# A graph layer, a mixture of experts and a second graph layer on one core: neighbouring tokens put side by side in a partition

## What is computed

```
x = x + (A @ (LN(x) @ W0 + b0)) / deg[:, None]          # A = adj != 0, deg = column sums
x = x + MoE(LN(x))        # 8 experts 256 -> 1024 -> 256, gelu, top 2 of a softmax gate
x = x + relu(D^-1/2 (A + I) D^-1/2 @ LN(x) @ WL.T + bL)
x = x + nibble_shift(LN(x))   # reads columns 0, 39, 40, 64..111, adds to columns 128..159
```

## Time and profile before

| | us |
|---|---|
| median of 3 runs | 1022.38 |
| the profiled execution, its own time | 1022.8 |
| its span, first to last instruction | 1021.0 |
| TensorE busy in the span | 929.0 |

### The profile page before, as it was taken

How to read it: one execution, slowest core, us unless ns; L and a number is a source line. 1 busy time by engine, 2 the same in 40 slices (tenths; PEclk the granted TensorE clock), 3 DMA queues, 4 the chain that set the end, 5 groups by cost and what they waited for, 6 DMA issues and landing times. The chain is left out here.

```text
span 1021.0 us, 21671 instructions
## 1 busy us (share of the span) xinstructions
PE 929.0 (91%) x6625; PEld 608.5 (60%) x6626; DVE 590.0 (58%) x1878; ACT 400.7 (39%) x837; POOL 429.6 (42%) x437
## 2 busy tenths in 40 slices
PE   8999899999913899999999999999379999999994
PEld 4354444444502799989989889899234454444442
DVE  6641996866698755655655655656256151251644
ACT  5858669576796443232232232233012101010111
POOL 3463746425576245545545545545444400210110
PEclk9999999999955999999999999999789999999997
DMA  9988899899786423323322332333299979775770
GB/s 324 411 290 312 317 335 351 289 337 382 249 284 182 160 45 48 54 46 47 54 45 47 53 47 46 53 47 46 44 336 402 370 230 327 266 263 166 242 259 26
DMA packets 91577, 199.92 MB, mean 196 GB/s; under 512 B 14241, under 2 KB 47266, under 8 KB 91394
## 3 DMA queue, kind: packets, MB, share of 16 engines
q1 hardware_dynamic: 74482, 168.37, 46.7%
q0 software_dynamic: 17040, 30.87, 14.8%
HBM read 177.05 MB, written 22.16 MB: 195 GB/s over the span
## 5 line engine op out<-in xcount | busy, mean ns | idle before, releaser
L1043 PE MATMUL bank<-adj_f,feat 128*128 128x512 f16 x1024 | 240.0, 389 | 5.2 <-DMA adj_f<-in_adjT 3.8
L1329 ACT ACTIVATE act_f<-bank,b_sb 128x256 f32<-128x256 f32 (+1 forms) x312 | 122.2, 449 | 255.4 <-PE bank L1260 255.4
L1260 PE MATMUL bank<-rT,experts 128*128 128x256 f16 (+1 forms) x1872 | 189.6, 262 | 2.5 <-DVE rT L1368 2.5
L1272 PE MATMUL bank<-experts,act_h 128*128 (+1 forms) x1680 | 189.1, 273 | 0.0
L1730 PE MATMUL bank<-adj_g,feat 128*128 128x512 f16 x768 | 179.7, 388 | 1.2 <-POOL feat L1556 1.2
L1260 PEld LDWEIGHTS bank<-rT,experts 128*128 (+1 forms) x1872 | 167.2, 98 | 19.8 <-DVE rT L1368 2.9
L1043 PEld LDWEIGHTS bank<-adj_f,feat 128*128 128x128 f16 x1024 | 97.1, 96 | 130.9 <-DMA adj_f<-in_adjT 6.0
L1272 PEld LDWEIGHTS bank<-experts,act_h 128*128 128x128 f16 x1680 | 163.0, 98 | 18.2
L925 ACT ACTIVATE spent<-adj_f 128x1024 f16<-128x1024 f32 x128 | 135.1, 1055 | 32.3 <-DMA adj_f<-in_adjT 27.1
L1187 POOL DMA_INDIRECT x_rows<-y,token x70 | 115.8, 1655 | 67.9 <-issue 58.2
L1730 PEld LDWEIGHTS bank<-adj_g,feat 128*128 128x128 f16 x768 | 74.4, 97 | 94.5 <-issue 2.1
(11 more groups left out here) (274 smaller groups left out, 978.5 us busy)
## 6 DMA issues: line engine op xcount, KB each, us to landing
adj_f<-in_adjT SPq DMA_DIRECT2D x128, 512.0 KB, 7.0
adj_g<-in_adjT SPq DMA_DIRECT2D x72, 512.0 KB, 6.0
adj_early<-in_adjT SPq DMA_DIRECT2D x24, 512.0 KB, 7.3
adj_g<-in_adjT SPq DMA_DIRECT2D x48, 256.0 KB, 3.1
unit_f<-in_W SPq DMA_DIRECT2D x16, 512.0 KB, 7.2
stage<-in_W SPq DMA_DIRECT2D x12, 512.0 KB, 6.5
x_ring<-in_x POOLq DMA_DIRECT2D x16, 256.0 KB, 7.1
x_rows<-agg SPq DMA_DIRECT2D x4, 1024.0 KB, 8.9
```

Of the source, the lines that this page charges most:

```text
L1043: last = pe.matmul(mine(s)[ib * DC + c][:, :], feat0[:, j, h, c * P:(c + 1) * P], adj_0[j % RING][:, ib * HALF_SWEEP:(ib + 1) * HALF_SWEEP ...
L1260: last = pe.matmul(pb[2 + q][:, k * SLOT + at:k * SLOT + at + width], w1_part(mine_e * DC + (f // FQ * W2_UNIT0 + c), wh)[:, (f % FQ) * P: ...
L1272: last = pe.matmul(pb[6 + r][:, 0:D], act_h[:, ah, f, r * P:(r + 1) * P], experts[:, ds(e[r] * DC + (W2_UNIT0 + f // UH), 1), wh, (f % UH) ...
L1329: last = a.activation(act_f[q][:, k, at:at + width], pb[2 + q][:, k * SLOT + at:k * SLOT + at + width], ACT.Gelu, bias=b1_sb[:, ds(mine_e ...
```

## The change

Tiles are grouped by four (`TOGETHER`), and partition p of tile 4 m + t holds token 512 m + 4 p + t. So for one partition four tiles are four neighbouring rows. Loads of `x` and stores of `out` take four rows of a partition as one run of 4 KB (two rows, 2 KB, in the pairs of L492). A tile j of the adjacency takes every fourth row of `adjT`; its buffer has the columns in their old order, so where 128 output tokens of one tile are needed, every fourth column is taken (`columns_of`): as weights in `project`, and for the self loop's square block. The kernel's own tables `x_rows` and `ln_rows` are kept in another order: row p * 16 + n of each half holds partition p of tile n, so eight tiles of `x_rows` are 8 KB in one run; a row of `ln_rows` is 1056 bytes of which 1024 are written, so its rows stay apart. The numbers in `val_i` follow that order. `mix` is stored by two DMAs in place of one. On GpSimd's queue the second gate half moves ahead of the split of W1's unit 2.

```
+TOGETHER = 4
+    def tokens_of(table, at, tiles):
+        grouped = table.rearrange("(m p t) d -> p m t d", p=P, t=TOGETHER)
+        if tiles < TOGETHER:
+            return grouped[:, at // TOGETHER, at % TOGETHER:at % TOGETHER + tiles, :]
+        return grouped[:, at // TOGETHER:(at + tiles) // TOGETHER, :, :]
+    def stored(table, at, tiles):
+        half = at // (NT // 2)
+        rows_of = table[half * (T // 2):(half + 1) * (T // 2), :].rearrange("(p n) d -> p n d", p=P)
+        return rows_of[:, at % (NT // 2):at % (NT // 2) + tiles, :]
+    def in_tiles(memory, tiles):
+        return memory if tiles < TOGETHER else memory.rearrange("p (m t) d -> p m t d", t=TOGETHER)
+    def columns_of(k):
+        first = k // TOGETHER * (TOGETHER * P) + k % TOGETHER
+        return slice(first, first + (P - 1) * TOGETHER + 1, TOGETHER)
+    def adj_rows(j, columns):
+        grouped = adjT.rearrange("(m p t) i -> p m t i", p=P, t=TOGETHER)
+        return grouped[:, j // TOGETHER, j % TOGETHER, columns]
...
-                sp.dma_start(agg[:, at:at + tiles, :], x_v[:, at:at + tiles, :]).then_inc(sem(f"x_loaded{g}"), 16)
+                sp.dma_start(in_tiles(agg[:, at:at + tiles, :], tiles), tokens_of(x, at, tiles)).then_inc(sem(f"x_loaded{g}"), 16)
...
-                    sp.dma_start(adj_f[j % RING][:, :], adj_v[j, :, s * SWEEP:(s + 1) * SWEEP]).then_inc(sem(f"adj_full{j % RING}"), 16)
+                    sp.dma_start(adj_f[j % RING][:, :], adj_rows(j, slice(s * SWEEP, (s + 1) * SWEEP))).then_inc(sem(f"adj_full{j % RING}"), 16)
...
-                sp.dma_start(x_rows[g * G * P:(g + 1) * G * P, :].rearrange("(n p) d -> p n d", p=P), agg[:, g * G:(g + 1) * G, :]
+                sp.dma_start(stored(x_rows, g * G, G), agg[:, g * G:(g + 1) * G, :]
...
-            sp.dma_start(ln_rows[0:T, D:ROW].rearrange("(n p) d -> p n d", p=P), mix[:, :, :]
-                         ).then_inc(sem("mix_stored"), 16)
+            for at in (0, NT // 2):
+                sp.dma_start(stored(ln_rows, at, NT // 2)[:, :, D:ROW], mix[:, at:at + NT // 2, :]).then_inc(sem("mix_stored"), 16)
...
-            pool.iota(val_i[:, 0:NT // 2], [[P, NT // 2]], base=-T // 2, channel_multiplier=1).then_inc(sem("numbers_set"), 1)
+            pool.iota(val_i[:, 0:NT // 2], [[1, NT // 2]], base=-T // 2, channel_multiplier=NT // 2).then_inc(sem("numbers_set"), 1)
...
             load_gate_rows(0)
-            split_unit(2)
             pool.wait_ge(sem("wg_half_turned"), 1)
             load_gate_rows(1)
-            for u in range(3, W2_UNIT0):
+            for u in range(2, W2_UNIT0):
                 split_unit(u)
...
-                project(pe, bank[:, 0:W0C], sum_hi, sum_lo, slice(k * P, (k + 1) * P), w0s, W0C).then_inc(sem("agg_ps_ready"), 1)
+                project(pe, bank[:, 0:W0C], sum_hi, sum_lo, columns_of(k), w0s, W0C).then_inc(sem("agg_ps_ready"), 1)
...
-                sp.dma_start(x_sb[:, at:at + tiles, :], x2_v[:, at:at + tiles, :]).then_inc(sem(f"x_loaded{g}"), 16)
+                sp.dma_start(x_sb[:, at:at + tiles, :], stored(x_rows, at, tiles)).then_inc(sem(f"x_loaded{g}"), 16)
...
-                square_block = adj_g[slot_of(s, t)][:, k * P:(k + 1) * P]
+                square_block = adj_g[slot_of(s, t)][:, columns_of(k)]
```

More of the change, by code:

```diff
@@ L322, in place @@
         return rows_early[:, n % 4, :] if n < NT // 2 else rows_late[:, n - NT // 2, :]
-    def out_row(n, first_tile, tiles, table):
-        return table[n * P:(n + tiles) * P, :].rearrange("(n p) d -> p n d", p=P)
     def over_tiles(ap):
@@ L391, in store_rows @@
                 k = g * G - NT // 2
-                sp.dma_start(ln_rows[g * G * P:(g + 1) * G * P, 0:D].rearrange("(n p) d -> p n d", p=P), rows_late[:, k:k + G, :].bitcast(F32)
+                sp.dma_start(stored(ln_rows, g * G, G)[:, :, 0:D], rows_late[:, k:k + G, :].bitcast(F32)
                              ).then_inc(sem("late_stored"), 16)
@@ L425, in _ @@
             sp.wait_ge(sem("mix_ready"), 1)
-            sp.dma_start(ln_rows[0:T, D:ROW].rearrange("(n p) d -> p n d", p=P), mix[:, :, :]
-                         ).then_inc(sem("mix_stored"), 16)
+            for at in (0, NT // 2):
+                sp.dma_start(stored(ln_rows, at, NT // 2)[:, :, D:ROW], mix[:, at:at + NT // 2, :]).then_inc(sem("mix_stored"), 16)
             sp.wait_ge(sem("x1_stored"), 16 * NG)
             sp.wait_ge(sem("late_stored"), 16 * 2)
-            sp.wait_ge(sem("mix_stored"), 16)
+            sp.wait_ge(sem("mix_stored"), 32)
         @block.gpsimd
@@ L440, in _ @@
             pool.memset(ones[:, :], 1.0).then_inc(sem("ones_set"), 1)
[L441 to L442 removed]
+            pool.iota(val_i[:, 0:NT // 2], [[1, NT // 2]], base=-T // 2, channel_multiplier=NT // 2).then_inc(sem("numbers_set"), 1)
+            pool.iota(val_i[:, NT // 2:NT], [[1, NT // 2]], base=1, channel_multiplier=NT // 2).then_inc(sem("numbers_set"), 1)
             pool.iota(count_i[:, :], [[1, P]], base=0, channel_multiplier=0).then_inc(sem("numbers_set"), 1)
@@ L491, in load_x_again @@
                 k = 2 * m % G
-                pool.dma_start(x_ring[:, k:k + 2, :], x_v[:, 2 * m:2 * m + 2, :]).then_inc(sem(f"x_again{m % (G // 2)}"), 16)
+                pool.dma_start(in_tiles(x_ring[:, k:k + 2, :], 2), tokens_of(x, 2 * m, 2)).then_inc(sem(f"x_again{m % (G // 2)}"), 16)
             def low_row(n):
@@ L500, in store_pair @@
                 pool.wait_ge(sem("rows_lo_ready"), n + 2)
-                pool.dma_start(ln_rows[n * P:(n + 2) * P, 0:D].rearrange("(n p) d -> p n d", p=P), rows_early[:, n % 4:n % 4 + 2, :].bitcast(F32)
+                pool.dma_start(stored(ln_rows, n, 2)[:, :, 0:D], rows_early[:, n % 4:n % 4 + 2, :].bitcast(F32)
                                ).then_inc(sem(f"early_stored{n // 2 % 2}"), 16)
@@ L533, in _ @@
                                     ).then_inc(sem("warmed"), 16)
-            pool.wait_ge(sem("mix_stored"), 16)
+            pool.wait_ge(sem("mix_stored"), 32)
             pool.wait_ge(sem("tokens_ready"), 1)
@@ L1179, in _ @@
             for j in range(EARLY):
-                sp.dma_start(adj_early[j][:, :], adj_v[j, :, 0:SWEEP]).then_inc(sem(f"adj_g_full{j}"), 16)
+                sp.dma_start(adj_early[j][:, :], adj_rows(j, slice(0, SWEEP))).then_inc(sem(f"adj_g_full{j}"), 16)
         @block.gpsimd
@@ L1476, in program @@
     add32 = w("add32", [P, G, 2, 16], F32)
-    out_v = out.rearrange("(n p) d -> p n d", p=P)
-    x2_v = x_rows[0:T, :].rearrange("(n p) d -> p n d", p=P)
     MARK, OP_SHL, OP_SHR, ALU_LO, OUTPUT_LO = 0, 39, 40, 64, 128
@@ L1515, in load_tile @@
                 sp.wait_ge(sem("adj_g_used"), s * NT + j + 1)
-                sp.dma_start(adj_g[slot_of(s, j)][:, 0:tiles * P], adj_v[j, :, at * P:(at + tiles) * P]
+                sp.dma_start(adj_g[slot_of(s, j)][:, 0:tiles * P], adj_rows(j, slice(at * P, (at + tiles) * P))
                              ).then_inc(sem(f"adj_g_full{slot_of(s, j)}"), 16)
@@ L1532, in _ @@
                     sp.wait_ge(sem("out_ready"), LAST_GROUP + 1)
-                sp.dma_start(out_v[:, at:at + tiles, lo:hi], made[LAST_GROUP % 2][:, 0:tiles, lo:hi]).then_inc(sem("last_stored"), 16)
+                sp.dma_start(tokens_of(out[:, lo:hi], at, tiles), in_tiles(made[LAST_GROUP % 2][:, 0:tiles, lo:hi], tiles)).then_inc(sem("last_stored"), 16)
             sp.wait_ge(sem("last_stored"), 48)
@@ L1548, in store @@
                 pool.wait_ge(sem("out_ready"), s + 1)
-                pool.dma_start(out_v[:, at:at + tiles, :], made[s % 2][:, 0:tiles, :]).then_inc(sem(f"out_stored{s % 2}"), 16)
+                pool.dma_start(tokens_of(out, at, tiles), in_tiles(made[s % 2][:, 0:tiles, :], tiles)).then_inc(sem(f"out_stored{s % 2}"), 16)
             pool.sem_inc(sem("feat_ready"), 2)
@@ L1735, in rows_out @@
             def rows_out(s, k):
-                project(pe, bank_of(s, k)[:, 0:D], agg_hi, agg_lo, slice(k * P, (k + 1) * P), wLs, D).then_inc(sem("proj_ps_ready"), 1)
+                project(pe, bank_of(s, k)[:, 0:D], agg_hi, agg_lo, columns_of(k), wLs, D).then_inc(sem("proj_ps_ready"), 1)
             for s in range(len(GROUPS)):
```

2 lines of the change are left out of this document (removed).

## The result

The changed kernel takes 1017.41 us (median of five runs, 1015.21 to 1018.14) beside 1022.44 for the one before on the same chip (1021.75 to 1023.65): a ratio of 0.9947 with a 95% interval of 0.9932 to 0.9961. The forecast was 1017.2. The profiled execution took 1018.14 us, its span is 1016.3; before it was 1022.8 and 1021.0, so the traces differ by 4.66 us.

What follows compares the result with a forecast made beforehand. TensorE, busy 91% of the span, was taken as the bound. Terms -4.95 - 0.6 - 0.1 + 0.5 = -5.15 us gave 1017.2 us against 1022.38; own range 1014.5 to 1019.5 (70%), overall range 1013.5 to 1023.

Steps and rivals of the forecast that it cites:

- The gate term, -4.95: Sweep 1 projections: issuing gate half 1 earlier removes the fifth's 3.33 us delay and the slow clock behind it, -4.95 us.
- The 7 us of cover: Gate chain in sweep 1: half 1 summed by 96.6, VectorE's first bank needed empty only by 103.66, so 7 us spare.
- The start of x, -0.6: First sweep: larger x runs shorten the early waits for adjacency tiles; -0.6 us taken, ends 0.4 and 1.8.
- x_sb, -0.1: Load of the first `x_sb` piece, 512 KB, after the last expert: larger runs gain 0.07 us, taken as -0.1.
- The self loop, +0.5: GpSimd's two strided instructions per tile, in the chain preparing the first tiles: +0.5 us; 1.2 by the skill's rule.
- The weights, no cost: Projection matmuls' weights from every fourth column: loads stay hidden, nothing taken; 30 us if 191 ns and not hidden.
- The tables and mix: Two stores of `mix` have 4 us of cover; gathers of spread rows have 1.08 us spare: no cost.
- from there the pace is normal again: Sweep 1 after the sixth projection, 4.95 us late: no further delay was claimed from that point.
- The gain is not given back through adjacency loads: Denies a rival: new L1043 waits for adjacency tiles return some 4 of the 4.95 us, about 1021.5, 10%.
- a share that rises while GB/s do not: Sign that the prediction is wrong: the DMA share rises without more GB/s; no size given.
- The pitch: Adjacency loads 64 KB apart: no change taken; rival of slower loads, +5.5 us, 1028, 9%; skill's rule 1.2 us in sweep 0.
- Strided weights and spread gathers: Rival: projection weight loads not hidden, 1047, or 35 expert slots lengthened by 1 us through growing landings, likewise; 4%.

Runs made afterwards that it cites:

- experiment 1: Kernel before with only the second gate half moved ahead of the split of unit 2: 1017.49 us, ratio 0.9953.
- experiments 2 and 4: First: changed kernel with the old gate order, 1020.02 us. Second: kernel before with only the first load of x in 4 KB runs, 1033.09 us, total not comparable.
- experiment 5: Kernel before with only the adjacency tiles taking every fourth row, 64 KB apart: 1031.68 us, total not comparable because the routing differs.
- experiment 7: Changed kernel with GpSimd's self-loop instructions moved off the chain of the second pass's first eight tiles: 1014.36 us, again 1015.03.
- the filler: Kernel of experiment 7 with 14 matmuls, whose result nothing reads, in TensorE's wait in the second expert slot: 1013.5 us, ratio 0.991.

## Why the prediction was right

- **The gate term, -4.95.** Right, and the sole large one: the wait and the clock behind it went, the difference between the first and the sixth projection is 4.93 us, and experiment 1 gives -4.8 in the median. The issue came at 82.17 and not 84.5, because half 0 was turned earlier (80.75 against 83.31), and half 1 took 8.7 us until its turn where 8 were allowed. The 7 us of cover were 7.7, from the first emptied bank at 94.89 to the fifth projection at 102.54. What the forecast took for a fixed consequence, the slow clock behind the wait, is not one: two of five traces with the wait don't have it (experiments 2 and 4). Read from one of these, the same working would have given -3.35. That the trace of before had the slow clock is luck; the median of experiment 1 bears the larger number out.
- **The start of x, -0.6.** Too small: -1.14 in this trace, and in the five other traces with the layout -1.2 to -1.7 against experiment 1's trace, or -1.7 to -2.2 against that of before. The three waits for tiles fell from 3.8 to 2.9 us. This is the term that was mis-sized. Its stated reason, the 1 KB runs, explains only half of the window's rate, and neither the runs nor the pitch alone is seen to bring the tile at 25 us earlier (experiments 4 and 5). It had a range of 0.4 to 1.8, and the trace of after lies in the middle of it.
- **x_sb, -0.1.** From the last slot (718.44 before, 713.02 after) to the landing it is 0.28 us shorter. But the traces of one order differ by more than this: 26.89 to 27.50 us in seven with the old order of the rows, 26.43 to 27.16 in six with the new one. The pieces of 1 MB behind it landed later (15.4 us against 13.1), with no wait of TensorE for them.
- **The self loop, +0.5.** 0.65 at tile 8, of which 4 instructions by 0.06 are 0.24. Another 0.34 lie between VectorE's scaling of tile 3 and that of tile 4 (4.14 us before, 4.48 after), where its small instructions beside GpSimd's took longer; why was not tried. The rule of the Trainium skill (GPSIMD Engine Reference, "Performance pitfalls for Q7 kernels"), by which 0.46 would be 0.7, an estimate from that page, does not hold here: 0.52 was measured. The prediction's sum by that rule is also wrong: 4 instructions by 0.24 are 1.0 us, not 1.2.
- **The weights, no cost.** Right: 113 to 118 ns against 96 to 102 for a load, hidden.
- **The tables and mix.** Right: two stores landed in 8.4 us against 9.1. The spare before a gather in the earlier trace rows was 1.08 and is 0.94 us in the same slot; over all slots GpSimd's waits for VectorE there were 13.1 us and are 20.7:

```profile
499.88 1.01 POOL L362 DMA_INDIRECT rows<-ln_rows,token  x1 [0.94 <-DVE gates L1382]
```

- **Not foreseen.** The slow clock at 338 us (+1.54). In return the wait of the third slot for its gather, 0.91 us in before, was covered, so that 0.46 is left of it in the table. In the forecast "from there the pace is normal again" was said of what follows the sixth projection, and TensorE's waits for other engines in the second stage were left out as unchanged. They are, but the clock behind them isn't. The forecast met the time in part by luck: this loss of 0.46 stood against 0.54 that the start brought beyond its term.
- **The rivals.** The gain is not given back through adjacency loads: no tile of a later sweep is waited for, though the DMA share from 111 to 116 us is now 1.05 at 361 GB/s. One of the prediction's signs of being wrong, a share that rises while GB/s do not, is there from 84 to 92 us (1.01 at 367 against 0.99 at 377), but TensorE is busy all through it. The pitch costs nothing that the first stage shows (experiment 5). The Trainium skill's table on the pitch (DMA: Bandwidth & Descriptors, "Latency and other measured facts") speaks of pitches from 512 KiB on, which no run here has. The 1.2 us that the prediction worked out from it for 64 KB did not come: 93.10 us against 93.17 to 93.98 for the first projection. Strided weights and spread gathers did not become the bound.

## What to carry to other kernels

Most of the gain came from one moved load: it alone brought 4.8 us, the whole change 5.0 and 5.6. Read the chain in order of time behind each single wait of the engine that bounds the kernel, and look for a load that stands on a queue behind something it doesn't need. Larger packets are worth only what an engine waits for them, here one or two us at the start of the first stage, and how much of it reaches the total is not settled. A price of half a microsecond in the chain that feeds the first tiles of a stage can be moved off it, as in experiment 7, if its inputs lie there before the chain begins. And before a stretch at the lower clock is counted as the price of a wait, look for it in a second trace.

## What was not expected of the hardware

- The same wait of TensorE is followed by a stretch at half clock in some executions and not in others: behind the 3.2 us at 104 us in three of five traces, behind the 2.45 us of the second slot in seven of the twelve without the filler (and in one of the two of experiment 7's program), behind the 2.01 us before the last group's projections in seven of thirteen. The group behind the wait takes about 1.6 us longer then. What this costs depends on what comes next: all of it at 107 us, 0.5 to 1.1 us in the second slot, where a wait for a gather is covered by it, and over 1 us at the end. Two traces of one program can differ by this much.
- 128 runs of 4 KB that start 64 KB apart were fetched no slower than runs 16 KB apart, and from 4.5 to 8 us, with x among them, at 341 GB/s against 240.
- GpSimd reading and writing every fourth float32 column takes 0.52 to 0.55 us for 128x128 (means of 24 instructions) against 0.46, 14% to 20% more; TensorE's weight load from every fourth float16 column 113 to 118 ns against 96 to 102.
